# Graph-transformer kernel: degree products with moving columns 8 bytes apart, and eight PSUM banks for the first expert chunk

## What is computed

```python
xn = layernorm(x)
x = x + gcn(xn, src, dst) + attention_mix(xn)
x = x + experts(layernorm(x))       # 8 experts, softmax gate, batch norm, two hidden layers of 256

def gcn(features, src, dst):
    out_deg = segment_sum(ones, src)
    in_deg = segment_sum(ones, dst)
    x = features * rsqrt(max(out_deg, 1)) @ W_gcn           # 256 -> 64
    agg = segment_sum(x[src], dst)
    return relu(agg * rsqrt(max(in_deg, 1)) + b) @ W_out + b_out
```

## Time and profile before

| | us |
|---|---|
| median of 3 runs | 4489.13 (4483.42 to 4490.09) |
| profiled execution, its own time | 4484.99 |
| its span, first to last instruction | 4483.3 |
| PE busy | 3576.9 (80%) |
| DVE busy | 3140.5 (70%) |
| POOL busy | 2788.0 (62%) |
| ACT busy | 2405.0 (54%) |

### The profile page before, as it was taken

One profiled execution on the slowest core, in us unless ns is written; L12 is line 12 of the kernel. 1 busy time (PEld: TensorE's weight loads), 2 busy tenths in 40 slices (PEclk: granted clock), 3 DMA queues, 4 the chain that ended last, 5 costly groups with the idle time before them and its releaser, 6 DMA issues. The chain is left out here.

```text
span 4483.3 us, 67252 instructions
## 1 busy us (share of the span) xinstructions
PE 3576.9 (80%) x17779; PEld 2293.6 (51%) x17779; DVE 3140.5 (70%) x10032; ACT 2405.0 (54%) x5559; POOL 2788.0 (62%) x2880
## 2 busy tenths in 40 slices
PE   6697889999999998678878778855277777777763
PEld 6654556666666665444444445534144444444442
DVE  7676566565655654788888888875567777777777
ACT  7243223333233333489999974434466666666664
POOL 0175577676665400377777777764777777777774
PEclk9998999999999999899999999975589989898986
DMA  3233122121221101555555555534222222222221
GB/s 100 69 95 107 38 48 47 34 46 34 44 43 30 31 1 37 158 138 145 144 143 142 143 151 161 159 94 117 33 40 40 40 39 41 39 40 39 40 39 28
DMA packets 291737, 331.29 MB, mean 74 GB/s; under 512 B 80182, under 2 KB 246062, under 8 KB 291366
## 3 DMA queue, kind: packets, MB, share of 16 engines
q0 software_dynamic: 105328, 175.77, 19.2%
q1 hardware_dynamic: 186038, 151.23, 12.4%
HBM read 289.56 MB, written 30.77 MB: 71 GB/s over the span
## 5 line engine op out<-in xcount | busy, mean ns | idle before, releaser
L3108 POOL DMA_INDIRECT st_rows<-tabr,router_rsrc x1072 | 1030.3, 961 | 329.8 <-issue 317.0
L2438 POOL DMA_INDIRECT all_XT<-tab,graph_gsrc x880 | 843.7, 959 | 268.1 <-issue 233.3
L1455 POOL DMA_INDIRECT st_rows<-tab,graph_gsrc x748 | 733.1, 980 | 393.2 <-issue 205.1
L1704 ACT ACTIVATE st_h<-st_ph,st_shift,st_scale 128x448 f32<-128x448 f32 x448 | 323.9, 723 | 744.6 <-PE st_ph L1566 744.3
L2468 PE MATMUL st_po<-all_XT,st_hot 128*128 128x264 f32 x1760 | 517.7, 441 | 108.2 <-DVE gat_sum L2678 105.4
L3165 PE MATMUL st_py<-st_w,st_hid 128*128 128x256 f32 x1568 | 440.9, 430 | 2.8 <-ACT st_hid L3213 2.8
L2468 PEld LDWEIGHTS st_po<-all_XT,st_hot 128*128 128x128 f32 x1760 | 300.3, 202 | 249.1 <-issue 114.3
L2678 DVE TENSOR_TENSOR gat_sum<-gat_sum,st_po 128x264 f32 x880 | 375.8, 427 | 70.9 <-PE st_po L2468 1.7
L3153 PE MATMUL st_px<-all_XT,st_w 128*128 128x512 f32 (+2 forms) x832 | 390.8, 616 | 14.8 <-ACT st_hid L3213 14.8
L3127 PE MATMUL st_pad<-st_adr,st_hott 128*128 x1072 | 68.0, 175 | 405.5 <-DVE st_zd L3279 393.0
L1579 PE MATMUL st_po<-all_XT,st_h 128*128 128x256 f32 x1568 | 371.0, 385 | 8.5 <-DVE all_X L1895 6.7
(11 more groups left out here) (519 smaller groups left out, 7337.2 us busy)
## 6 DMA issues: line engine op xcount, KB each, us to landing
st_bc<-drowr SPq DMA_DIRECT2D x268, 128.0 KB
st_bc<-drow SPq DMA_DIRECT2D x220, 128.0 KB
st_rows<-tabr,router_rsrc POOLq DMA_INDIRECT x1072
all_XT<-tab,graph_gsrc POOLq DMA_INDIRECT x880
st_xtb<-xtd SPq DMA_DIRECT2D x98, 128.0 KB
st_rows<-tab,graph_gsrc POOLq DMA_INDIRECT x748
tab<-gat_sum SPq DMA_DIRECT2D x7, 924.0 KB
xtd<-all_XT SPq DMA_DIRECT2D x49, 128.0 KB, 1.7
```

Of the source, the lines that this page charges most:

```text
L1455: g.indirect_dma_start(self.rows[:, b, u, :], None, self.R.tab0, bass.IndirectOffsetOnAxis(self.R.gsrc[:, t:t + 1], 0)).then_inc(self.s_ro ...
L1704: a.activation((self.h1, self.h2)[l][:, fb, h * HALF:(h + 1) * HALF], self.ph[:, m % 3, 0:HALF], ACT.Relu, bias=self.shift[:, l, i:i + 1], ...
L2438: g.indirect_dma_start(self.rows[:, b, u, :], None, self.R.tab1, bass.IndirectOffsetOnAxis(self.R.gsrc[:, t:t + 1], 0)).then_inc(self.s_ro ...
L3108: g.indirect_dma_start(self.rows[:, b, u, :], None, self.R.tabr, bass.IndirectOffsetOnAxis(self.R.rsrc[:, t:t + 1], 0)).then_inc(self.s_ro ...
```

## The change

Front: `ohhi` is laid out as four quads of four columns, `[quad, window, 4]`, so that the 49 moving columns of a product lie 4 numbers (8 bytes) apart. DVE writes it with one instruction as before, whose patterns have one dimension more. `ohlo` stays as it is.

Stage1, chunk 0 only: a table `FIRST` gives each side product a bank of its own (the three `ph`, two `pe`, two `po` and `side`), and where a bank is used a second time, the use whose release PE has to wait for. In ACT's program `degree_root(0)` moves ahead of the four `mixed(0, q)`. Chunks 1 to 6 are as before.

```diff
@@ class Front
-        self.ohhi = f.sb("ohhi", [P, 2, W, self.BAT], BF16)
+        self.ohhi = f.sb("ohhi", [P, 2, self.QUADS, W, 4], BF16)
...
-                mm = t.matmul(self.deg[:, 0:W], self.ohlo[:, h % 2, :, b], self.ohhi[:, h % 2, :, b], start=False,
-                              stop=False, skip_group_check=True)
+                mm = t.matmul(self.deg[:, 0:W], self.ohlo[:, h % 2, :, b], self.ohhi[:, h % 2, b // 4, :, b % 4],
+                              start=False, stop=False, skip_group_check=True)
...
-            v.tensor_tensor(self.ohhi[:, h % 2], self.count[:, 0:W, :],
-                            self.hi[:, col:col + self.BAT].unsqueeze(1).to_broadcast([P, W, self.BAT]),
+            quads = [P, self.QUADS, W, 4]
+            v.tensor_tensor(self.ohhi[:, h % 2], self.count[:, 0:W, 0:4].unsqueeze(1).to_broadcast(quads),
+                            self.hi[:, col:col + self.BAT].rearrange("p (q b) -> p q b", b=4).unsqueeze(2).to_broadcast(quads),
                             ALU.is_equal).then_inc(self.s_hot, 1)
@@ class Stage1
+    FIRST = {("mix", 0): ("ph", 0, None), ("mix", 1): ("ph", 1, None), ("mix", 2): ("ph", 2, None),
+             ("mix", 3): ("side", 0, None), ("ht", 0): ("pe", 0, None), ("ht", 1): ("pe", 1, None),
+             ("y", 0): ("po", 0, None), ("y", 1): ("po", 1, None), ("y", 2): ("ph", 0, ("mix", 0)),
+             ("y", 3): ("ph", 1, ("mix", 1)), ("xt", 0): ("po", 0, ("y", 0)), ("xt", 1): ("po", 1, ("y", 1)),
+             ("xt", 2): ("side", 0, ("mix", 3)), ("xt", 3): ("ph", 2, ("mix", 2)), ("lg", 0): ("side", 0, ("xt", 2))}
...
-            m = self.at[what, n, k]
-            if m:
-                sem, count = self.free[m - 1]
-                t.wait_ge(sem, count)
+            if n == 0 and (what, k) in self.FIRST:
+                before = self.FIRST[what, k][2]
+                if before:
+                    sem, count = self.free[self.at[before[0], 0, before[1]]]
+                    t.wait_ge(sem, count)
+                return
+            sem, count = self.free[self.at[what, n, k] - 1]
+            t.wait_ge(sem, count)
...
-                mm = t.matmul(self.side[:, 0:HALF], R.weff[:, c, fb * P:(fb + 1) * P],
+                mm = t.matmul(self.bank("mix", n, q)[:, 0:HALF], R.weff[:, c, fb * P:(fb + 1) * P],
...
+        degree_root(0)
         for q in range(4):
             mixed(0, q)
-        degree_root(0)
```

More of the change, by code:

```diff
@@ L550 @@
     HALVES = GB // BAT
+    QUADS = BAT // 4
     SETS = 2
@@ L1402, in __init__, with bank @@
                 self.free.append((self.s_sa, acts))
+    FIRST = {("mix", 0): ("ph", 0, None), ("mix", 1): ("ph", 1, None), ("mix", 2): ("ph", 2, None),
[4 rows of a table added]
+    def bank(self, what, n, k):
+        if n or (what, k) not in self.FIRST:
+            return self.side
+        where, b, _ = self.FIRST[what, k]
+        if where == "po":
+            return self.po[:, b].rearrange("p k d -> p (k d)")
+        return {"ph": self.ph, "pe": self.pe}[where][:, b] if where != "side" else self.side
     def windows(self, engine, n):
@@ L1498, in turn_sums @@
             for j in range(4 * k, min(4 * k + 4, TPI)):
-                mm = t.transpose(self.side[0:GCOL, (j - 4 * k) * P:(j - 4 * k + 1) * P], self.hf[:, j, :], R.ident[:, :])
+                mm = t.transpose(self.bank("ht", n, k)[0:GCOL, (j - 4 * k) * P:(j - 4 * k + 1) * P], self.hf[:, j, :],
+                                 R.ident[:, :])
             mm.then_inc(self.s_side, 1)
@@ L1506, in rest @@
             for j in self.pair(k):
-                o = self.side[:, (j - 2 * k) * D:(j - 2 * k + 1) * D]
+                o = self.bank("y", n, k)[:, (j - 2 * k) * D:(j - 2 * k + 1) * D]
                 for c in range(C):
@@ L1518, in turn_rows @@
                     o = (2 * (j - 2 * k) + c) * P
-                    mm = t.transpose(self.side[:, o:o + P], self.xn[:, j, c * P:(c + 1) * P], R.ident[:, :])
+                    mm = t.transpose(self.bank("xt", n, k)[:, o:o + P], self.xn[:, j, c * P:(c + 1) * P], R.ident[:, :])
             mm.then_inc(self.s_side, 1)
@@ L1654, in mixed @@
             fb, h = divmod(q, 2)
-            a.activation(self.hid[:, fb, h * HALF:(h + 1) * HALF], self.side[:, 0:HALF], ACT.Gelu,
+            a.activation(self.hid[:, fb, h * HALF:(h + 1) * HALF], self.bank("mix", n, q)[:, 0:HALF], ACT.Gelu,
                          bias=self.R.beff[:, fb:fb + 1]).then_inc(self.s_sa, 1)
@@ L1665, in sums_turned @@
             a.activation(self.ht[:, 4 * k:4 * k + m, :],
-                         self.side[0:GCOL, 0:m * P].rearrange("p (j t) -> p j t", j=m), ACT.Copy).then_inc(self.s_sa, 1)
+                         self.bank("ht", n, k)[0:GCOL, 0:m * P].rearrange("p (j t) -> p j t", j=m), ACT.Copy)\
+                .then_inc(self.s_sa, 1)
         def spread_root(n):
@@ L1675, in rows_turned @@
             a.activation(self.xt[:, :, 2 * k * P:(2 * k + m) * P].rearrange("p c (j t) -> p j c t", j=m),
-                         self.side[:, 0:m * C * P].rearrange("p (j c t) -> p j c t", j=m, c=C), ACT.Copy)\
+                         self.bank("xt", n, k)[:, 0:m * C * P].rearrange("p (j c t) -> p j c t", j=m, c=C), ACT.Copy)\
                 .then_inc(self.s_sa, 1)
@@ L1819, in take_rest @@
                 for j in self.pair(k):
-                    v.tensor_tensor(x(n, j), x(n, j), self.side[:, (j - 2 * k) * D:(j - 2 * k + 1) * D], ALU.add)\
+                    v.tensor_tensor(x(n, j), x(n, j), self.bank("y", n, k)[:, (j - 2 * k) * D:(j - 2 * k + 1) * D], ALU.add)\
                         .then_inc(self.s_x, 1)
```

## The result

The changed kernel takes **4458.95 us** (4453.25 to 4461.8, 4 runs) against 4487.0 in the same runs of the kernel before: ratio **0.9941, 95% interval 0.9929 to 0.9952**, 28 us faster. Forecast were 4460 us and a gain of 27.1. The profiled execution of the changed kernel took 4461.8 us, 2.9 above its median, with a span of 4460.0.

What follows compares the result with a forecast made beforehand. PE was taken to set the pace in two runs of Front's batches, and a one-bank chain to bound Stage1's start; 10.1 + 17.0 = 27.1 us off 4487.1 gave 4460 us, range 4449 to 4476.

Steps and rivals of the forecast that it cites:

- The bound by the loads: Front's degree products: loads of stationary columns 32 bytes apart allow one product per 52 to 67 ns, taken as 67.
- the 35 to 50 forecast: Front's degree products: the moving read falls from 97 to some 35 to 50 ns at 8 bytes apart.
- L394's 33 ns: Pace of L394's products, each with its load of columns 8 bytes apart; such a load takes 33 ns at most.
- the two terms, 33 and 34 ns: Front's load bound of 67 ns: 33 for a load at 8 bytes, 34 more for one at 32 bytes.
- The rival that the loads set 97 already: Front's products stay at 97 ns because the loads bind, Front keeps its length: 4470 us, chance 0.17.
- 10.1 us were forecast: Front's gain: 0.48 us per batch over the 21 batches on PE's path, 10.1 us.
- stretches that were put at nothing: Front until about 101 us (ACT's counting passes) and 132 to 160 us (DVE's sort): shorter products gain nothing.
- The term of 14.9 us to the last sum: Stage1's first chunk, mix through y: DVE takes the last sum at about 443.1 instead of 457.95, 14.9 us.
- The rival of the half clock in y: Stage1's first chunk: y's 42 matmuls run at half clock, 4469 us, chance 0.06.
- The xt term: Stage1's first chunk: xt's transposes and copies without hand-overs take 4.5 instead of 6.6 us, 2.1 us gained at half clock.
- The range's ends, 4449 and 4476: Whole kernel: loads at 97 ns or low clock one at a time; other side 18 + 17 = 35 us gained.
- The rival that ends slower: Front: DVE's second-table instruction over 1.0 us dearer, 1.56 instead of 0.56, so DVE bounds and the kernel slows; chance 0.03.

Runs made afterwards that it cites:

- loads_alone: The kernel before with the stationary columns of the degree products 8 bytes apart, the moving ones left at 32: 4487.3 us, ratio 1.0000.
- both_quads: The changed kernel with the stationary columns 8 bytes apart as well: 4450.8 us, ratio 0.9920 against the kernel before.
- moving_flat: The changed kernel with stationary columns 8 bytes apart and moving columns next to each other (2 bytes): 4492.7 us, ratio 1.0019 against the kernel before.
- root_back: The changed kernel with the degree root back behind the four Gelu steps, banks as changed: 4464.4 us, ratio 0.9955 against the kernel before.
- after_again: The changed kernel measured once more, nothing altered: 4459.4 us, ratio 0.9944 against the kernel before.
- stage1_alone: The kernel before with only the Stage1 edits (banks and moved degree root), Front as before: 4473.0 us, ratio 0.9968.
- front_alone: The kernel before with only the Front edits, Stage1's first chunk as before: 4478.4 us, ratio 0.9977.

## Why the prediction was right

**Part 1, the pace.** The bound by the loads was 52 to 67 ns, taken as 67; measured are 62.5, and loads_alone and both_quads show that the order of the bounds is right: the moving operand set 97, the loads set the pace now, the moving read at 8 bytes is at 48.75, inside the 35 to 50 forecast. The size is partly luck. L394's 33 ns and its record of 114 stand at the full clock, L701's 148 at half of it, as the last section shows; in Front itself the records differ by 148 - 127 = 21 (loads_alone), and moving_flat bounds a load of columns 8 bytes apart by 42.5 ns only. No run shows the two terms, 33 and 34 ns, one by one at Front's clock. Nor is a record the load's own time: the one forecast to stay near 148 rose to 170 with the load unchanged. The rival that the loads set 97 already falls, since shorter loads alone gain nothing. The Trainium skill's rule for loads (TensorE: Matmul & The Clock Gate, LDWEIGHTS), 107 ns for 128 columns, taken by itself would have allowed none of the paces of 62.5, 48.75 and 42.5 ns, each with a load.

**Part 1, the time.** 10.1 us were forecast, 11.3 measured at the last product. A batch saves 0.54 us instead of 0.48, over 52 batches 28 us of PE's work; 16.7 us of it went into longer waits for DVE (63.8 to 80.5), the rest, 11.4, came through. Not where the prediction had it, though: by the starts of the batches the lead over the kernel before was 2.4 us at the first batch of the first run (101.71 to 99.27), 6.3 at its last, 7.3 at the first of the second run and 10.8 at its last. The two runs gave 3.9 and 3.5 us over 10 and 9 rounds, where 0.48 a round makes 4.8 and 4.3, because PE stops for DVE in both of them now; and 3.4 us came in stretches that were put at nothing, those up to 101 us and from 132 to 160. That the sum agrees is partly luck. Front's end, forecast near 207 us, is at 204.6 by Prelude's first matmul (217.7 before). That DVE would be level with PE was in the text, and it is where more gain in PE alone stops. DVE's table at 559 ns was right (561).

**Part 2.** The term of 14.9 us to the last sum came out at 34.3 - 19.2 = 15.1: mix without stops, the transposes behind it, y at the full clock. The rival of the half clock in y did not come, and root_back shows what it hangs on: the 4.5 us stop ahead. The xt term was mis-sized: 2.1 us forecast at half clock, 3.2 measured (6.63 to 435.71 - 432.33 = 3.38), as the clock, half there before, was at 0.78 of full. In sum 18.4 in the first execution, 16.8 and 17.1 in after_again and stage1_alone, where mix ran longer at half the clock (its first twelve matmuls 7.44 and 7.08 us instead of 6.33): 17.0 was the middle.

**The sum.** 27.1 forecast, 28 measured, by two parts of about the size forecast. The range's ends, 4449 and 4476, lie some 3 and 6 us outside what its terms give (4487 - 35 = 4452 and 4470); the text does not say why. The rival that ends slower, DVE's table above 1.5 us, did not come by this change's layout, but moving_flat has just that price: 1.01 us more per table. By the prediction's account that is 52 x 1.01 - 16 = 36 us against 27 gained, 9 slower; its kernel is 0.19% slower than the one before, 8.5 us. That these meet so closely is partly chance, since moving_flat changes the loads as well.

## What to carry to other kernels

For small products with a load each, both operands' distance between columns is a price per product, and here the dearer of the two set the pace: change the one that binds, then look at the other, and let the engine that writes the table keep short runs in which every operand steps. In a chain through one bank, spreading the first turns over idle banks was worth what the stops cost, as far as the trace of the chain goes, and the order of the steps on the reading engine close to half of the whole there (7.5 to 9 of 17 to 18 us): a step whose result comes late goes ahead of the queue, where its table load lies beside matmuls. When PE gains, check at once who is busier in that stretch; here more than half of PE's saved work went into waits for DVE.

## What was not expected of the hardware

**The granted clock of Front's rows.** The windows say 1.00 in Front, before and after the change. But the clock's first record in these traces begins at 225.5 us in the kernel before and at 211.8 in the changed one; where there is none, the window reads 1.00. In front_alone, with the same code in Front and records from 134.2 us on, they say 0.50 in 145 to 160 us. The line of front_alone:

```profile
145.00:160.00 15.00, 11.36 (x111) 11.18 (x112) 13.67 (x27) 6.25 (x16) 6.98 (x5) 0.50 0.23 71
```

and that of the changed kernel:

```profile
145.00:160.00 15.00, 11.26 (x110) 11.08 (x111) 13.67 (x27) 6.17 (x16) 6.89 (x5) 1.00 0.24 71
```

The work in them takes the same time, and both end Front at the same place (last product 175.2 and 175.3). The transposes of L223 in the changed kernel, in Front and in the stage behind Stage1, ns min/median/max:

```profile
L223 PE MATMUL front_pt<-all_ident,all_XT x98: 418/421/476, 38.0 to 173.4; 128*128 128x128 f32 x98
...
L223 PE MATMUL tab_pt<-all_ident,tab_xn x98: 272/273/477, 1737.9 to 1830.2; 128*128 128x128 f32 x98
```

None of Front's 98 is faster than 418 ns (408 in the kernel before). So by its rows Front ran at 1.2 GHz here, whatever the column says; the forecast's paces of Front were paces at that level, and its 33 ns of L394 one at 2.4 GHz (granted 1.00 from 252 to 258 us, around the group of the earlier trace rows). In both_quads, which stops PE more, Front shows both levels, and the pace of 48.75 ns hardly differs between them.

**The distance between moving columns.** With stationary columns 8 bytes apart, 49 moving columns take 92.5 ns at 32 bytes, 50.6 at 8 and 42.5 at 2, all three at half the clock. The Trainium skill (SBUF — State Buffer, Specifications (TRN2)) asks for two hits in a 16-byte line for full bandwidth. Columns of 2 bytes, 8 apart, have two in each, and are within 8 ns of the contiguous ones; at 32 bytes apart none shares a line.

**A table's layout on DVE.** 784 numbers take 559 ns in runs of 16, 561 in runs of four and 1566 where one operand stands still along the run. The Trainium skill (VectorE: DVE Perf Modes, What auto-detection actually checks) ties a doubled rate (2x_1P) to 16-bit operands that all step by one; in the first two layouts they do, in the third they do not. A halved rate alone does not make 1566: with the prediction's 0.39 us for it, an estimate, the table would take 0.95 us. Whether the rest comes from the step of 32 bytes or from the operand that stands still, no run tells apart.
